# Delta spread by pairs of 64-row products, few-row products padded to 96 rows, B replicated later

## The reference

```
# 1. state-space layer, per sequence
h = layernorm(x) * gamma + beta
u, z = split(h @ in_proj.T)                 # 256 channels each
uc = silu(causal_conv(u, 4 taps) + conv_b)
dt, B, C = split(uc @ x_proj.T, [64, 16, 16])
delta = softplus(dt @ dt_proj.T + dt_b)     # 256 channels
state[c, n] = exp(delta[c] * A[c, n]) * state[c, n] + delta[c] * B[n] * uc[c]    # over the tokens
y[c] = sum_n state[c, n] * C[n] + D[c] * uc[c]
x = layernorm(x + (y * silu(z)) @ out_proj.T + x)
# 2. mixture of 8 experts, the best 2 of each token
p, e = top2(softmax(x @ Wg + bg))
x = layernorm(x + sum_k p_k * (gelu(x @ W1[e_k] + b1[e_k]) @ W2[e_k] + b2[e_k]))
```

## Time and profile before

| | |
|---|---|
| median of 3 runs | 893.62 us |
| profiled execution | 891.96 us, span 890.2 us |
| mean granted TensorE clock | 0.764 of 2.4 GHz |
| TensorE busy | 678.5 us, 76% |
| VectorE busy | 687.3 us, 77% |
| ScalarE busy | 423.3 us, 48% |
| GpSimd busy | 530.7 us, 60% |

### The profile page before, as it was taken

One profiled execution on the slowest core, in us unless ns is written; L12 is line 12 of the kernel. 1 busy time (PEld: TensorE's weight loads), 2 busy tenths in 40 slices (PEclk: granted clock), 3 DMA queues, 4 the chain that ended last, 5 costly groups with the idle time before them and its releaser, 6 DMA issues. The chain is left out here.

```text
span 890.2 us, 12242 instructions
## 1 busy us (share of the span) xinstructions
PE 678.5 (76%) x2905; PEld 311.1 (35%) x2905; DVE 687.3 (77%) x1350; ACT 423.3 (48%) x884; POOL 530.7 (60%) x526
## 2 busy tenths in 40 slices
PE   3768989878778988878888976878631998899920
PEld 2322222222222322222232221212221888888820
DVE  2167788989998897899889899999732677777754
ACT  3537458357465534735655453324110555455424
POOL 5124546745687757677676677867863455455433
PEclk9885867877987776787797666556555899999975
DMA  3074455565376855547465465655003666666646
GB/s 82 0 202 106 95 127 133 121 152 131 82 189 172 196 135 134 122 115 172 105 142 124 112 142 118 161 120 123 24 27 91 166 177 170 176 168 178 181 128 175
DMA packets 60390, 117.37 MB, mean 132 GB/s; under 512 B 8817, under 2 KB 37297, under 8 KB 52257
## 3 DMA queue, kind: packets, MB, share of 16 engines
q1 hardware_dynamic: 56000, 107.60, 49.4%
q0 software_dynamic: 4320, 8.99, 3.1%
HBM read 100.21 MB, written 16.35 MB: 131 GB/s over the span
## 5 line engine op out<-in xcount | busy, mean ns | idle before, releaser
L532 POOL TENSOR_TENSOR hc<-hs,Crep 128x1024 f32<-128x1024 f32 x128 | 300.1, 2355 | 188.2 <-PE bank L759 102.0
L1295 DVE TENSOR_TENSOR_SCAN hs<-bank,state,flow 128x512 f32<-128x512 f32 x256 | 314.6, 1268 | 58.5 <-ACT bank L1061 53.2
L1061 ACT ACTIVATE bank<-bank,negA 128x512 f32<-128x512 f32 x256 | 165.1, 662 | 253.4 <-PE bank L749 242.0
L749 PE MATMUL bank<-delta,sel 32*128 32x512 f32 x512 | 195.0, 839 | 83.3 <-DVE hs L1295 83.2
L1285 DVE TENSOR_TENSOR flow<-flow,bank 128x2048 f32<-128x2048 f32 x63 | 142.7, 2265 | 0.0
L749 PEld LDWEIGHTS bank<-delta,sel 32*128 32x128 f32 x512 | 50.8, 237 | 212.8 <-DVE hs L1295 145.4
L1189 ACT ACTIVATE flow<-bank,b1T 128x128 f32<-128x128 f32 x284 | 81.1, 369 | 79.8 <-PE bank L926 77.6
L759 PE MATMUL bank<-hc,kc 128*32 128x512 f32 x512 | 91.2, 795 | 6.1 <-POOL hc L532 6.1
L698 PE MATMUL bank<-hT,wtapT 128*128 128x512 f32 x128 | 88.9, 822 | 6.9 <-issue 4.9
L926 PE MATMUL bank<-flow 128*128 128x128 f32 x568 | 83.0, 291 | 14.0 <-issue 9.1
L641 POOL DMA_INDIRECT results<-flow,idn x71 | 69.9, 984 | 33.2 <-issue 31.4
(11 more groups left out here) (180 smaller groups left out, 774.8 us busy)
## 6 DMA issues: line engine op xcount, KB each, us to landing
flow<-du_d SPq DMA_DIRECT2D x63, 1024.0 KB, 7.1
flow<-L_ffn_W SPq DMA_DIRECT2D x71, 256.0 KB
xg<-xs SPq DMA_DIRECT2D x71, 66.0 KB
hs<-results SPq DMA_DIRECT2D x16, 256.0 KB, 4.8
du_d<-du SPq DMA_DIRECT2D x28, 128.0 KB, 3.1
xin<-L_attn_x SPq DMA_DIRECT2D x8, 256.0 KB, 3.1
out<-hc SPq DMA_DIRECT2D x8, 256.0 KB, 2.5
results<-flow,idn POOLq DMA_INDIRECT x71
```

The source lines that it names most:

```text
L532: nc.gpsimd.tensor_tensor(hc[:, Q % 2, two, :], hs[:, Q % 2, two, :], Crep[u % 3][:].unsqueeze(1).broadcast_to([P, 2, T]), ALU.mult).then_ ...
L749: ins = nc.tensor.matmul(dbank[i][:], sel[32 * i:32 * i + 32, q % 4, :], delta[u % 2][32 * i:32 * i + 32, q // 4, :])
L1061: nc.scalar.activation(dbank[G % 4][:], dbank[G % 4][:], ACT.Exp, scale=negA[:, ch:ch + 1]).then_inc(s_ex, 1)
L1295: nc.vector.tensor_tensor_scan(hs[:, Q % 2, j, :], dbank[G % 4][:], flow[Q % 3][:, j, :], state[:, Q // QUADS % 2, Q % QUADS, j:j + 1], AL ...
```

## The change

- `spread_pair` now takes rows 0 to 63 for one product and rows 64 to 127 for the other. `sel` has two variants (`odd`), each with ones only in one 32-row block of each half and zeros in the other. So one call serves tiles 0 and 2 of a quad, the next tiles 1 and 3; `ORDER` gives scans and decays this order, and `times_c` takes every second tile.
- `spread_b`, `spread_c` and `proj_dt` contract all 96 rows of `xdbl`; the weights' added rows are zero.
- `spread_b` moves from step 29 to the end of step 31, behind `add_states`.
- ScalarE does `c_evac` before `one_plus` (L1037) in step 5, and no longer in step 6.
- The zeros of `sel`, `bcs` and `wdtT` are written by VectorE at the start; GpSimd's memset of `sel` goes.

```diff
-        sel = sb("sel", [P, 4, P])
+        sel = sb("sel", [P, 2, 4, P])
-        wdtT = sb("wdtT", [RANK, HALVES, P])
+        wdtT = sb("wdtT", [XP, HALVES, P])
...
-                two = slice(2 * pair, 2 * pair + 2)
+                two = slice(pair, 4, 2)
...
-            link(nc.gpsimd.memset(sel[:], 0.0))
+            pool.wait_ge(s_zero, 6)
             for p in range(4):
-                rows = sel[32 * p:32 * p + 32, :, :].rearrange("r m (n c) -> r m n c", c=CH)
+                rows = sel[32 * p:32 * p + 32, p % 2, :, :].rearrange("r m (n c) -> r m n c", c=CH)
...
-                nc.tensor.matmul(o[:], bcs[RANK:XP, 1, :], xdbl[u % 2][RANK:XP, :]).then_inc(s_ff, 1)
+                nc.tensor.matmul(o[:], bcs[:, 1, :], xdbl[u % 2][:]).then_inc(s_ff, 1)
...
-                nc.tensor.matmul(o[:], wdtT[:, h, :], xdbl[u % 2][0:RANK, :]).then_inc(s_ff, 1)
+                nc.tensor.matmul(o[:], wdtT[:, h, :], xdbl[u % 2][:]).then_inc(s_ff, 1)
...
-                q, j = r // 2, 2 * (r % 2)
-                for i in (j, j + 1):
-                    ins = nc.tensor.matmul(dbank[i][:], sel[32 * i:32 * i + 32, q % 4, :],
-                                           delta[u % 2][32 * i:32 * i + 32, q // 4, :])
+                q, odd = r // 2, r % 2
+                for i in range(2):
+                    rows = slice(64 * i, 64 * i + 64)
+                    ins = nc.tensor.matmul(dbank[2 * odd + i][:], sel[rows, odd, q % 4, :], delta[u % 2][rows, q // 4, :])
...
-                    if g == 29 and late:
-                        spread_b(j + 1)
...
+                    if late and g == 31:
+                        spread_b(j + 1)
...
-                ch = tile_of(g // 4, g % 4)
+                ch = tile_of(g // 4, ORDER[g % 4])
...
+            nc.vector.memset(sel[:], 0.0).then_inc(s_zero, 1)
+            nc.vector.memset(bcs[0:RANK], 0.0).then_inc(s_zero, 1)
+            nc.vector.memset(wdtT[RANK:XP], 0.0).then_inc(s_zero, 1)
```

More of the change, by code:

```diff
@@ L21 @@
 CH = P // N
+ORDER = (0, 2, 1, 3)
 QUADS = 8
@@ L675, in _ @@
             pe.wait_ge(s_pe, 8)
-            pe.wait_ge(s_k, 8)
+            pe.wait_ge(s_k, 7)
+            pe.wait_ge(s_zero, 6)
             def front_bank(u, what):
@@ L737, in spread_b @@
                 after(pe, s_bu, QUADS * u)
-                nc.tensor.matmul(Brep[:], bcs[RANK:XP, 0, :], xdbl[u % 2][RANK:XP, :]).then_inc(s_br, 1)
+                nc.tensor.matmul(Brep[:], bcs[:, 0, :], xdbl[u % 2][:]).then_inc(s_br, 1)
             def spread_pair(R):
@@ L817, in host @@
                         first_host(g)
+                        if g == 31:
+                            spread_b(1)
                         continue
@@ L959, in setup @@
                 nc.scalar.copy(wxpT[:].rearrange("p h c -> p (h c)"), bank[3][:, 0:2 * XP]).then_inc(s_pe, 1)
-                nc.scalar.copy(wdtT[:].rearrange("p h c -> p (h c)"), bank[3][0:RANK, 256:512]).then_inc(s_pe, 1)
+                nc.scalar.copy(wdtT[0:RANK].rearrange("p h c -> p (h c)"), bank[3][0:RANK, 256:512]).then_inc(s_pe, 1)
                 nc.scalar.copy(b1T[:], bank[4][:, 32:64]).then_inc(s_pe, 1)
@@ L1105, in host @@
                         if g == 5:
+                            c_evac(j + 1)
                             one_plus(j + 1)
-                        if g == 6:
-                            c_evac(j + 1)
                         if g == 8:
@@ L1288, in scan @@
             def scan(G):
-                Q, j = G // 4, G % 4
+                Q, j = G // 4, ORDER[G % 4]
                 dve.wait_ge(s_ex, G + 1)
-                if j == 0:
+                if G % 4 == 0:
                     dve.wait_ge(s_bu, Q + 1)
@@ L1400, in _ @@
             nc.vector.tensor_copy(run[:], base).then_inc(s_zero, 1)
-            dve.wait_ge(s_zero, 4)
+            dve.wait_ge(s_zero, 7)
             second_h()
```

## The result

The changed kernel takes 859.13 us (median of 4 runs, 857.12 to 864.88) against 894.91 us of the kernel before on the same chip: a ratio of 0.961 (95% interval 0.956 to 0.967), 35.8 us less. Forecast were 866 us, 28 us less. The profiled span went from 890.2 to 855.3 us.

A forecast was written before the change was run, and what follows sets the result against it. VectorE sets the unit stage's pace, idling 53.2 us for decays behind a slow-clocked TensorE. Returns 34.9 + 0.6 (start) + 0.5 (stage end) - 4 - 4 = 28.0 us; 893.6 - 28 = 865.6, said as 866 us, range 854 to 887.

The forecast's parts named there:

- Rival 1: Unit stage: TensorE's clock stays as it is, only the moves in order count; 8 us less, 885.6 us; chance 0.18.
- this inference: TensorE in the unit stage: products that leave rows empty keep the clock down; pairs filling 128 rows raise it.
- Rival 3: `spread_pair`: the two 64-row products run one after the other, 1.12 us more per pair; 907 us; chance 0.09.
- the unit ends: Step 30: seven VectorE waits for decays, 19.9 us together, of which 16 were to come back.
- steps 7 and 9: Eight VectorE waits, 10.3 us together, near the transposes' wait for `c_evac`; 8 us were to come back.
- step 28: Five VectorE waits behind ScalarE's silu and its two table loads, 5.5 us together; 1.9 us were to come back.
- the first unit: Five VectorE waits, 11.7 us together, at 1.2 GHz with fronts and pairs packed closely; 8 us were to come back.
- the other 5.8 us: The rest of VectorE's 53.2 us of waits for decays; 1 us was to come back.
- the inflow that would wait for `spread_b`: Unit starts: VectorE's inflow waits for `spread_b` right before it; cost taken as 4 us, bounds 0 and 14.
- a return of the slow clock: Second half of the unit stage: VectorE catches up and meets TensorE's next slow stretch; cost taken as 4 us.
- the signs named: Unit stage: mean clock 0.85 or more, pair 1.13 us, decay waits about 25 us, new inflow wait about 0.5 us.
- The start: Kernel start: GpSimd's memset of `sel` goes, the affine_selects end near 18.7 instead of 19.3 us; 0.6 us less.

The follow-up runs named there:

- the first experiment: The changed kernel with each product of a pair contracting only its own 32 rows again, all else as changed: 882.98 us, ratio 0.983 to the kernel before.
- the run that forces it: The changed kernel with each product of a pair contracting all 128 rows, one after the other: 868.93 us, ratio 0.967 to the kernel before.

## Why the prediction was right, point by point

*The clock follows the rows in use.* Shown: only the contracted rows were changed in the first experiment, and the stage's clock went from 0.85 to 0.75; with 128 rows in turn it was 0.94. No run separates the number of rows from the form of the product, a 32-, 64- or 128-row one. The stage of the kernel before had 0.72; the 0.77 of the prediction is one unit's. Rival 1, the clock unmoved, is refuted by the changed kernel's 0.85; the share of the moves in order was 0.5%, less than its price. The rows of before carried this inference less well than the prediction has it: in its 10.2 us at 1.2 GHz, convolutions and z, which contract 128 rows, take 5.9 us and the two pairs 4.0. The guess was right, and the first experiment is what shows it.

*The pair keeps its time.* 1.13 us measured, as taken. Rival 3 didn't occur, and the run that forces it is faster than before by 3.3% with a pair of 1.96 us, above the 1.9 at which the rival was to decide. Its price took 66 us of TensorE per unit and 12 us of waits for banks, 78 together. The run has 456.6 us of work in 8 units, 57 each, and 91.0 us of waits for scans, 11.4 each. So the waits were right and the work was too high: the unit of the earlier trace rows holds more of it than the average (481.5 us at 0.72 are 43 us per unit at full clock, not 48), and the pair costs 0.83 us more, not 1.12.

*Places.* The terms of the sum against VectorE's waits in the profile after: at the unit ends I took back 16 of 19.9 us, and one wait of 1.16 is left of seven; at steps 7 and 9, 8 of 10.3, and 2.9 in four waits are left; at step 28 (counted from 0 it is scan 27), 1.9 of 5.5, and 3.9 is left in five, four of 0.74 and one of 0.99; in the first unit 8 of 11.7, and 5.7 is left in two waits; of the other 5.8 I took back 1, and 0.5 is left. So the unit ends gave 2.7 us more than taken, the rest 4.3 more, the first unit 2.0 less, and all together 39.0 instead of 34.9.

*What returned them.* The prediction calls all of these what a higher clock returns. For the largest term, the unit ends, that is only half of it. With the moves alone, at the old clock, 17.3 of the 19.9 us are gone; what the clock adds is that the inflow no longer waits 10.4 us for `spread_b` in exchange.

*Costs.* I gave 4 us to the inflow that would wait for `spread_b`: no such wait is in the stage of the changed kernel, while it is 10.7 us in six waits with 32-row pairs. I gave another 4 to a return of the slow clock: VectorE's waits don't show it. And I didn't see `oh`, 10.1 us, against 4.2 us that `delta` and `taken` gave. That these net 5.9 us come near my 8 is luck. The earlier trace rows can't show a blocked operation, since it counts as busy.

*The sum.* 28.0 us were forecast and the profiled execution is 34.9 shorter: 4.1 us are returns taken too low, 2.1 are costs taken too high, and the rest, 0.7, isn't traced. Of the signs named, the wait for decays fell to 14.2 us, below the 25, the inflow's wait of 0.5 didn't appear, and the transposes' waits for the copy of C fell from 23.1 us in eight to 4.4 in four, 1.1 each, as forecast. One reading was off without harm: 256 scans of 1.268 and 63 inflows of 2.265 us are 467 us, and 457 is their busy time, in which scans that overlap count once.

*The start.* The affine_selects end at 18.7 instead of 19.3 us, as forecast.

*What I had not argued.* That the parts need each other. The stages of five kernels, without and with either half (the first four have no padding; us in the stage, from the groups and waits of each profile):

| | clock | waits for decays | inflow for `spread_b` | `oh` | ratio |
|---|---|---|---|---|---|
| before | 0.72 | 53.2 | 0 | 5.2 | 1 |
| moves alone | 0.72 | 28.9 | 10.4 | 12.2 | 0.995 |
| 64-row pairs alone | 0.82 | 43.2 | 0 | 12.0 | 0.989 |
| both | 0.84 | 16.2 | 1.0 | 16.2 | 0.963 |
| both, padded (the change) | 0.85 | 14.2 | 0 | 15.3 | 0.961 |

The halves give 0.5% and 1.1%, both together 3.7%. My rivals treated clock and order as shares that add. With the pairs alone, the pair at step 30 waits for a product that itself waits for VectorE, and no clock shortens that. With the moves alone, the order is free of it, and TensorE at 1.2 GHz is what the inflow waits for instead. And either half already loses some 7 us to `oh`, where both together lose 11.

## What to carry to other kernels

When TensorE is busy all the time and its clock is low, look at the rows that its products use: the same products over more rows, side by side where they can be, came out faster here, with no more time per pair. Faster work on one engine pays only where the order lets it: look for a product that waits for the bottleneck engine ahead of one that this engine waits for, and put table swaps where the bottleneck has a long operation of its own (here this took 8 us of waits away, though the time isn't told apart). And compare the busy time of small operations too: one of 0.2 us took 2.8 beside a multiplication on another engine.

## What the runs showed of the hardware

- Products of 64 rows in the two halves of the array run side by side: 1.13 us for two of float32 with 512 columns at 2.4 GHz, against 1.96 for two of 128 rows.
- Rows that meet only zeros in the 0/1 matrix lifted the clock all the same: 0.85 against 0.75 in the stage, though they add nothing to the product's sums. Whether they would with zeros on the side of `delta`, no run shows.
- A VectorE operation with both inputs in SBUF (`oh`) took up to 2.83 us instead of 0.2 beside a GpSimd multiplication of 2.37 us (3.08 with the pairs alone), and ended within 0.1 us of it. Beside GpSimd's indirect DMAs it took 0.20 to 0.28. The Trainium skill ("SBUF — State Buffer", Summary: rules for kernel authors) says that when VectorE has two SBUF inputs while the GpSimd operation reads SBUF, the second of the two to issue is blocked until the first has finished; the ends agree. That VectorE's record starts 0.32 us before GpSimd's (0.62 with the pairs alone) does not fit its order of issue, and what happened in these 0.32 us stays open; GpSimd had an indirect DMA until 332.75.
